# Attention rows through memory in a perceiver layer on one Trainium2 core

## The reference

```python
def _layernorm(x): return (x - mean(x)) / sqrt(var(x) + eps)

def xattn(query, key, value):                       # 16 heads of 16
    Q, K, V = heads(query @ Wq.T + bq), heads(key @ Wk.T + bk), heads(value @ Wv.T + bv)
    scores = softmax(einsum('bhsd,bhtd->bhst', Q, K) / sqrt(16), axis=-1)
    out = einsum('bhst,bhtd->bhsd', scores, V)
    out = out.reshape(B, T_src, D_MODEL)            # (b, h, s, d) read as rows, heads not put back
    return out @ Wh.T + bh

def attn(x):                                        # random features, causal sums
    q, k, v = split(x @ Wqkv + bqkv)
    qf, kf = features(q), features(k)               # normalise, project, clip, exp
    ctx = einsum(qf, cumsum(kf x v)); den = maximum(einsum(qf, cumsum(kf)), 1e-6)
    out = (ctx / den).transpose(0, 2, 1, 3).reshape(B, T, C)
    return out @ Wout + bout

def ffn(x): return (silu(x @ wg.T) * (x @ wu.T)) @ wd.T

x = x + xattn(_layernorm(x), ctx_1024, ctx_1024)
x = x + attn(_layernorm(x))
x = x + ffn(_layernorm(x))                          # weights int / 127
```

## Time and profile before

| | |
|---|---|
| median of three runs | 876.47 us |
| profiled execution | 875.48 us, span 873.8 us |
| PE busy | 829.1 us (95%) |
| ACT busy | 541.5 us (62%) |
| DVE busy | 417.2 us (48%) |
| granted PE clock, mean | 0.99 |
| mean DMA rate | 137 GB/s |

### The profile page before, as it was taken

How to read it: one execution, slowest core, us unless ns; L and a number is a source line. 1 busy time by engine, 2 the same in 40 slices (tenths; PEclk the granted TensorE clock), 3 DMA queues, 4 the chain that set the end, 5 groups by cost and what they waited for, 6 DMA issues and landing times.

```text
span 873.8 us, 20543 instructions
## 1 busy us (share of the span) xinstructions
PE 829.1 (95%) x8817; PEld 569.8 (65%) x8817; DVE 417.2 (48%) x746; ACT 541.5 (62%) x598; POOL 47.1 (5%) x76
## 2 busy tenths in 40 slices
PE   6899999999999998999999998999999999989876
PEld 5666666666666666676666665667666666657656
DVE  7433236444644445534654446354474444402654
ACT  2478887776577665667567764575657666672141
POOL 1034000000000000000000000000000000000010
PEclk9899999999999999999999999999999999999999
DMA  7486654646344333346343441443614333202000
GB/s 248 172 258 237 241 183 166 209 158 193 122 146 146 142 125 133 122 133 191 136 146 145 146 142 53 158 158 129 195 65 170 122 122 119 100 2 50 0 2 15
DMA packets 58768, 120.08 MB, mean 137 GB/s; under 512 B 21552, under 2 KB 29744, under 8 KB 55152
## 3 DMA queue, kind: packets, MB, share of 16 engines
q1 hardware_dynamic: 56880, 114.31, 38.3%
q0 software_dynamic: 1792, 4.40, 1.7%
HBM read 78.84 MB, written 37.75 MB: 133 GB/s over the span
## 4 chain that ended last, share of the span: by engine, by line
PE 82%; DVE 8%; issue 4%; DMA 2%; ACT 2%; DVEq 1%; POOL 1%; SPq 0%; POOLq 0%; ACTq 0%
PE ps_o L816 26%; PE ps_s L828 18%; PE ps_pa L662 10%; PE ps_pa L617 10%; PE ps_pa L763 2%; PE ps_pa L692 2%; PE ps_pa L788 2%; PE ps_pa L775 2%; PE ps_pa L754 1%; ACT probs L1258 1%; PE ps_pa L740 1%; DMA oscr<-y 1%; PE ps_pa L684 1%; PE ps_pa L795 1%; PE ps_pa L767 1%
## 5 line engine op out<-in xcount | busy, mean ns | idle before, releaser
L1258 ACT ACTIVATE probs<-ps_s 128x1024 f32<-128x1024 f32 x512 | 496.8, 1023 | 234.2 <-PE ps_s L828 227.7
L816 PE MATMUL ps_o<-probs,values 128*17 128x256 f32 x4096 | 256.1, 385 | 0.0
L828 PEld LDWEIGHTS ps_s<-qstack,kstack 64*128 64x128 f32 x2048 | 140.0, 186 | 99.6 <-ACT probs L1258 48.8
L828 PE MATMUL ps_s<-qstack,kstack 64*128 64x256 f32 x2048 | 194.0, 307 | 5.3 <-ACT probs L1258 5.3
L816 PEld LDWEIGHTS ps_o<-probs,values 128*17 128x17 f32 x4096 | 104.1, 98 | 98.7 <-issue 9.8
L1343 DVE TENSOR_SCALAR kparts<-ps_pa,b_heads 128x512 fp32r<-128x512 f32 x64 | 48.0, 750 | 107.4 <-PE ps_pa L617 107.1
L662 PE MATMUL ps_pa<-wv_hi,ctx_hi 128*128 128x256 f32 x256 | 79.6, 311 | 2.9 <-DVE wv_lo L1331 2.2
L1360 DVE TENSOR_TENSOR values<-ps_pa,bv_pair 128x512 f32<-128x512 f32 x64 | 44.2, 690 | 77.5 <-PE ps_pa L662 77.1
L662 PE MATMUL ps_pa<-wv_lo,ctx_hi 128*128 128x256 f32 x256 | 72.5, 283 | 0.0
L662 PE MATMUL ps_pa<-wv_hi,ctx_lo 128*128 128x256 f32 x256 | 72.4, 283 | 0.0
L617 PE MATMUL ps_pa<-ctx_hi,wk_hi 128*128 128x512 f32 x128 | 56.4, 441 | 0.0
(11 more groups left out here) (274 smaller groups left out, 786.7 us busy)
## 6 DMA issues: line engine op xcount, KB each, us to landing
kstack<-kscr SPq DMA_DIRECT2D x96, 512.0 KB, 5.3
kscr<-kparts SPq DMA_DIRECT2D x64, 512.0 KB, 2.7
ctx_raw<-ctxT SPq DMA_DIRECT2D x32, 512.0 KB, 6.5
qstack<-qscr SPq DMA_DIRECT2D x12, 256.0 KB, 3.5
qscr<-qparts SPq DMA_DIRECT2D x4, 512.0 KB, 3.1
xh<-x SPq DMA_DIRECT2D x4, 256.0 KB, 5.4
kstack<-kstack SPq DMA_DIRECT2D x2, 512.0 KB, 6.0
qstack<-ksample SPq DMA_DIRECT2D x4, 256.0 KB, 3.6
```

The costliest lines, as they stand in the source:

```text
L816: last = mm(ps_o[32 * j:32 * j + DH + 1, g * S:(g + 1) * S], values[par][:, i, head_of_step(g, j), :], prob[:, j * S:(j + 1) * S], start=b ...
L828: last = mm(ps_s[s % 2][:, j * S:(j + 1) * S], kstack[par][rows, u, i * P:(i + 1) * P], queries[rows, u, :], start=True, stop=True)
L1258: nc.scalar.activation(probs[n % AHEAD][:, :], ps_s[n % 2][:, :], ACT.Exp, scale=float(DH) ** -0.5).then_inc(fast["exp_done"], 1)
```

## The change

Stages: `oT0`, `oT1`, `o2T0`, `o2T1`, `y2T` go. `on` (step 9) and `o2n` (92) come, both on DVE alone. The softmax output is written from `o_sb` as it is, denominator included, one DMA for each of the four row groups of 17 partitions, and read back with the queries as rows; DVE divides after the read. The linear output takes the same way, and is read back by dimension and head, denominators repeated, so that it is already transposed: `wout`'s rows are reordered to match, in eight loads of the weight instead of one. `wh` and `wout` signal after the addition; the layernorms are stages `ln1` and `ln2` of their own. `ln0T` goes from 94 to 92, `q` from 100 to 98, `wout` from 92 to 94, `ln2T` from 96 to 99, `gu0` from 99 to 100, and ACT takes the gates up to one exponential earlier. In the last tail the first two transposes are gone, SP and ACT write two groups each, and down uses the hidden columns in two fp32r parts that DVE cuts.

```diff
-AT = {"o": 1, "oT0": 3, "oT1": 4, "yT": 12, "wh": 13, "ln1T": 19, ...
+AT = {"o": 1, "on": 9, "yT": 12, "wh": 13, "ln1": 13, "ln1T": 19, ...
-      ... "pv3": 84, "o2T0": 86, "o2T1": 88, "y2T": 90, "wout": 92,
-      "ln2T": 96, "gu0": 99, "gate0": 101, ...
+      ... "pv3": 84, "o2n": 92, "wout": 94, "ln2": 94,
+      "ln2T": 99, "gu0": 100, "gate0": 101, ...
-HEAD_AT = {"ln0": 86, "ln0T": 94, "q": 100, ...
+HEAD_AT = {"ln0": 86, "ln0T": 92, "q": 98, ...
-ACT_BEHIND = {n: 1 - AT[n] % 2 if AT[n] // QUAD in WIDE_QUADS else QUAD - 1 - AT[n] % QUAD for n in FEATS + GATES}
+ACT_BEHIND = {n: 1 - AT[n] % 2 if AT[n] // QUAD in WIDE_QUADS else QUAD - 1 - AT[n] % QUAD for n in FEATS}
+ACT_BEHIND.update({n: (QUAD - 2 if AT[n] % QUAD < 2 else QUAD - 1) - AT[n] % QUAD for n in GATES})
-        oscr = scratch("oscr", [H, S, DH], FP32)
+        o2scr = scratch("o2scr", [DH + 1, H, S], FP32)
+        oscr = scratch("oscr", [ST, DH + 1, HALF, S], FP32)
+        def write_heads(eng, c, j):
+            t, e = j // CI, j % CI
+            eng.dma_start(oscr[t].rearrange("d (g e) s -> e d g s", e=CI)[e],
+                          o_sb[32 * j:32 * j + DH + 1, :, :]).then_inc(c["o_written"], 16)
...
+            def read_rows(t, landed):
+                sp.dma_start(o_rows[:, t, :, :], oscr[t].rearrange("d h (a u) -> (h a) d u", u=DH)).then_inc(landed, 16)
+            def regroup_output(c, tails):
+                wait_all((c["o_written"], tails * (16 * GH) + 16 * GH))
                 for t in range(ST):
+                    read_rows(t, c["o_in"])
+            def turn_values(c, clock, tails):
+                wait_all((c["operand"], c.at("operand", clock, "pv3")))
+                for j in range(GH):
+                    sp.dma_start(o2scr.rearrange("d (g j) s -> j d g s", j=GH)[j],
+                                 o_sb[32 * j:32 * j + DH + 1, :, :]).then_inc(c["o2_written"], 16)
+                wait_all((c["o2_written"], tails * (16 * GH) + 16 * GH))
+                sp.dma_start(o2_den, o2scr[DH:DH + 1].to_broadcast([P // H, H, S])).then_inc(c["o2_in"], 16)
+                sp.dma_start(o2_rows, o2scr[0:DH].rearrange("(i e) h s -> (e h) i s", i=CI)).then_inc(c["o2_in"], 16)
...
+                    if b and p == AT["pv3"] // STEPS:
+                        turn_values(fast, tail_of(b - 1), b - 1)
...
+            warm(ps_p, 34)
             for t in range(ST):
-                pe.wait_ge(*vector_of("o0"))
-                for g in range(G):
-                    if g == G // 2:
-                        pe.wait_ge(*scalar_of("o1"))
-                    last = nc.tensor.transpose(halves[t][:, g * P:(g + 1) * P], o_sb[:, g, t * P:(t + 1) * P], ident[:, :])
-                last.then_inc(last_product, 1)
-            warm(ps_p, 12)
...
-            warm(ps_p, 26)
...
+                pe.wait_ge(*vector_of(f"y{t}"))
+                turn_rows(halves[2 + t], t, y).then_inc(last_product, 1)
...
+                    for part in range(2):
+                        last = mm((ps_p, ps_a)[t][:, 0:D], last_part(k, part)[:, t * P:(t + 1) * P], wd_r[:, k, :],
+                                  start=k + part == 0, stop=k + part == HB)
...
-            for dst, src in ((wh_sb, whT), (wout_sb, wout)):
-                pool.dma_start(dst[:, :, :], wr(src)).then_inc(late_in, 16)
+            pool.dma_start(wh_sb[:, :, :], wr(whT)).then_inc(late_in, 16)
+            for e in range(P // H):
+                pool.dma_start(wout_sb[e * H:(e + 1) * H, :, :], wout.rearrange("(h i e) n -> e h i n", i=CI, e=P // H)[e]
+                               ).then_inc(late_in, 16)
...
+            for j in range(CI, GH):
+                write_heads(act, fast, j)
...
+            def scaled_rows(t):
+                return v.tensor_tensor(y[:, t, :].rearrange("p (u d) -> p d u", d=DH), o_rows[:, t, 0:DH, :],
+                                       rden[:, t, :].unsqueeze(1).to_broadcast([P, DH, DH]), ALU.mult)
...
+                elif name == "on":
+                    dve.wait_ge(c["o_in"], clock[1] * (16 * ST) + 16 * ST)
+                    if c is fast and tails:
+                        dve.wait_ge(c["stored"], tails * 16)
+                    v.reciprocal(rden[:, :, :], o_rows[:, :, DH, :])
+                    check_rows()
+                    for t in range(ST):
+                        last = scaled_rows(t)
+                elif name == "o2n":
+                    dve.wait_ge(c["o2_in"], clock[1] * 32 + 32)
+                    v.tensor_scalar(o2_den, o2_den, 1e-6, None, ALU.max)
+                    dve.drain()
+                    v.reciprocal(o2_den, o2_den)
+                    dve.drain()
+                    last = v.tensor_tensor(xT[:, :, :], o2_rows, o2_den.unsqueeze(1).to_broadcast([P, CI, S]), ALU.mult)
                 elif name in ("wh", "wout"):
-                    v.tensor_tensor(xs[:, :, :], xs[:, :, :], bank[:, :].rearrange("p (t d) -> p t d", t=ST), ALU.add)
-                    dve.drain()
+                    last = v.tensor_tensor(xs[:, :, :], xs[:, :, :], bank[:, :].rearrange("p (t d) -> p t d", t=ST), ALU.add)
+                elif name in ("ln1", "ln2"):
                     last = layernorm(c, name, clock)
...
+            for t, landed in enumerate(((fast["o_in"], (B - 1) * (16 * ST) + 16), (o_in_last, 16))):
+                dve.wait_ge(*landed)
+                v.reciprocal(rden[:, t, :], o_rows[:, t, DH, :])
+                dve.drain()
+                scaled_rows(t).then_inc(last_vector, 1)
...
-                v.scalar_tensor_tensor(hid[:, k, :], gate_e[:, k % 2, :], 1.0, hid[:, k, :], ALU.add, ALU.mult
-                                       ).then_inc(last_vector, 1)
+                v.scalar_tensor_tensor(hid[:, k, :], gate_e[:, k % 2, :], 1.0, hid[:, k, :], ALU.add, ALU.mult)
+                dve.drain()
+                if k >= HALF // 2:
+                    dve.wait_ge(*product_of(f"gu{HB - 1}"))
+                cut(last_part(k, 0), last_part(k, 1), hid[:, k, :]).then_inc(last_vector, 1)
```

More of the change, by code:

```diff
@@ L542, in _ @@
             load_x(fast, B - 1, (fast["operand"], fast.at("operand", tail_of(B - 2), "down")))
-            for t in range(ST):
-                sp.wait_ge(*vector_of(f"y{t}"))
-                sp.dma_start(oscr[:, t * P:(t + 1) * P, :].rearrange("h s d -> s h d"),
-                             y[:, t, :].rearrange("p (h d) -> p h d", h=H)).then_inc(fast["o_written"], 16)
-            sp.wait_ge(fast["o_written"], B * 32)
+            sp.wait_ge(*vector_of("o0"))
+            sp.wait_ge(*scalar_of("o1"))
+            for j in range(CI):
+                write_heads(sp, fast, j)
+            sp.wait_ge(fast["o_written"], B * (16 * GH))
             for t, landed in enumerate((fast["o_in"], o_in_last)):
-                sp.dma_start(y[:, t, :], oscr[t * HALF:(t + 1) * HALF, :, :].rearrange("a (u s) d -> (a u) (s d)", u=S // DH)
-                             ).then_inc(landed, 16)
+                read_rows(t, landed)
             for t in range(ST):
@@ L723, in stage @@
                                   ident[:, :], start=True, stop=True, skip_group_check=True)
-                elif kind in ("oT", "o2T"):
-                    for g in range(G):
-                        last = nc.tensor.transpose(bank[:, g * P:(g + 1) * P], o_sb[:, g, n * P:(n + 1) * P],
-                                                   ident[:, :])
                 elif name == "yT":
-                    pe.wait_ge(c["o_in"], clock[1] * 16 + 16)
-                    last = transpose_blocks(bank, y)
-                elif name == "y2T":
                     last = transpose_blocks(bank, y)
@@ L786, in down_part @@
                 for t in range(ST):
-                    last = mm(bank[:, t * D:(t + 1) * D], hid[:, k, t * P:(t + 1) * P], wd_sb[:, k, :],
+                    last = mm(bank[:, t * D:(t + 1) * D], hid[:, k, t * P:(t + 1) * P], wd_r[:, k, :].bitcast(FP32),
                               start=k + t == 0, stop=k == HB - 1, skip_group_check=True)
@@ L1178, in _ @@
             pool.wait_ge(fast["k_stacked"][1], 3 * STACKED)
-            pool.dma_start(wd_sb[:, :, :].bitcast(INT32), wr(wdT)).then_inc(i_in, 16)
+            for k, part in zip((0, HB - CI), wd_int):
+                n = part.shape[1]
+                pool.dma_start(part, wr(wdT)[:, k:k + n, :]).then_inc(i_in, 16)
             def weighted(c, f, clock):
@@ L1412, in normalise @@
-                by_half = bank[:, :].rearrange("p (g a e c) -> p a g e c", a=CI, e=CI, c=32)
-                scale = rden[:, :].rearrange("p (g a e) -> p a g e", a=CI, e=CI)
-                for a in range(CI):
-                    last = v.tensor_tensor(y[:, t, a * P:(a + 1) * P].rearrange("p (g e d) -> p g e d", e=CI, d=DH),
-                                           by_half[:, a, :, :, 0:DH],
-                                           scale[:, a, :, :].unsqueeze(3).to_broadcast([P, G, CI, DH]), ALU.mult)
@@ L1418, in normalise @@
-                return last
```

(11 more changed lines are left out.)

141 lines of the change are left out of this document (50 added, 91 removed), and 4 rows, old and new, of the table AT.

## The result

| | median, us | lowest to highest | against before |
|---|---|---|---|
| before | 877.28 | 875.84 to 879.27 (4 runs) | |
| after | 958.25 | 957.4 to 959.67 (4 runs) | 1.0923, interval 1.0894 to 1.0951 |

The changed kernel is 81 us slower; the prediction was 965, with 860 to 985 as its range. The profiled execution took 957.4 us around a span of 955.7.

What follows compares the result with a forecast made beforehand. PE was taken to bound the kernel, busy 829.1 of 873.8 us. From 875.5, gains of 11.8 give 863.7; one-engine writes add 82 and six clock falls 20, making 965 us, range 860 to 985.

Steps and rivals of the forecast that it cites:

- One engine: Output writes: 17 partitions put each set on one DMA engine, 13.2 us a set, 82 us of waits together; chance 0.62.
- Clock falls: PE's long waits at six places in the tails: one clock fall each at 3.3 us, 20 us together.
- the 2.68 us stand: PE's stand in tail 1 of the kernel before, taken as the length beyond which the clock falls.
- The base, 863.7: Whole kernel if writes are as quick as those now: the parts sum to -11.8 us, giving 863.7 us.
- four writes go out at 198.4 and land near 202.7: Softmax rows in tail 0, spread writes: reads land at 207.9 and yT starts at 210.2, where it was.
- Setup: Batch 0: eight more weight loads on POOL at about 0.5 us each cost nothing, or 4 us once if uncovered.
- Rival 2: Tails: writes spread but late, PE standing 2 us longer at six places with clock falls, 895 us; chance 0.07.
- Sums and norms apart: ln0T in tails 0 and 1: stalls of 2.3 and 2.7 us go, and tail 1's clock fall of 3.3.
- The linear path: Late in the tails, with spread writes: wout can start at 537.4, PE wants it at 536.7, a 0.7 us stall.
- The reciprocal of 256 columns: DVE's o2n before wout: taken as 1.7 us if the excess is per column, 0.5 if fixed.
- The last batch: With spread writes wh could start 2.4 us earlier, but warming ends near 801 and a clock fall offsets it: 0.
- The gated stage: Last batch's gate and down products: DVE's four operations make a step of 1.86 us instead of 1.82, +2.7 us.

Runs made afterwards that it cites:

- e6: Changed kernel with 55 and 45 unused warming products filling PE's waits before yT and wout: 946.49 us, ratio 1.079.
- e9: Changed kernel with 32-partition writes, last batch's down product in fp32 and the softmax tail latest (on 12, yT 16): 881.93 us, ratio 1.0035.
- e2: Changed kernel with each write padded from 17 to 32 partitions, 15 of them rows nobody reads: 885.37 us, ratio 1.0077.
- e5: Kernel before with only sums and norms taken apart and ln0T moved ahead of wout, transposes kept: 868.34 us, ratio 0.9906.
- e10: Changed kernel with each write padded from 17 to 25 partitions: 899.35 us, ratio 1.0225.
- e3: Changed kernel with each write padded from 17 to 18 partitions, one row nobody reads: 884.86 us, ratio 1.0078.
- e8: Changed kernel with 32-partition writes, a later softmax tail (on 12, yT 14) and the last batch's down product in fp32: 878.75 us, ratio 1.0004.
- e11: Kernel before with sums and norms apart, and only the linear rows through memory in 32-partition writes: 868.14 us, ratio 0.9877.

## Why the prediction was right, and where its sizes were off

The step on which it rested, all 272 pieces of a set on one DMA engine, was right, and so was its cause, the count of 17. From one copy of o to the next, in the profiles, against the prediction's own terms (in each tail 12.2 and 11.0 us of waits and two clock falls, less what the tail gains):

| stretch | before | after | more | predicted |
|---|---|---|---|---|
| start to copy of o, batch 0 | 195.1 | 196.0 | 0.9 | 0 |
| to the next copy | 202.7 | 226.3 | 23.6 | 26.2 |
| to the next | 206.7 | 225.4 | 18.7 | 21.3 |
| to the last batch's | 192.4 | 216.8 | 24.4 | 27.4 |
| to the end | 76.8 | 91.1 | 14.3 | 14.8 |
| sum | 873.8 | 955.7 | 81.9 | 89.7 |

- **One engine.** Predicted 48 ns a piece (40 to 54) and 13.2 us a set; the windows give 43 ns, 11.7 us. PE stands 13.1 us before yT, where the 12.2 counted and the 1.1 by which PE is early make 13.3; 10.5 before wout, where 11.0 and the stall of 0.7 make 11.7; 11.5 before the last yT (12.1 for the chain). The sizes hold within 1.2 us, in part by luck: the set took less than thought, and the queueing ahead of it and the reads behind it more. Three slips in the working hardly matter to it: 272 pieces at 48 ns are 13.1 us, 40 ns take 15 us off the seven sets and not 17, and the old writes of y had 4,096 pieces of 64 B, not 4,352.
- **Clock falls.** 3.3 us each was too much; e6 gives 2.0. Over six this is 8 us, and it is nearly the whole distance between 965 and 958. This is the term of the total that was mis-sized: 3.3 was 3.0 of lost work in one stretch and an allowance for its edges. Why a fall costs less here was not shown. Nor is the 2.68 us stand a border: in e9 the clock fell behind a stand of 1.94.
- **The base, 863.7, was wrong as the time with spread writes, and it did not show in the total.** e2 has the spread writes and takes 885. What was wrong is "four writes go out at 198.4 and land near 202.7": they go out behind 1.5 MB for the key stack and 256 KB of xs, and it takes 7.9 us, not the 4.3 that a set takes with nothing ahead of it. Three tails at 4.0 us of wait and 2.0 of clock (e6's price, for a longer stand) are 18 of the 21 us. In e2's profile the three tails lie 6.1, 6.7 and 7.3 us above the prediction's stretches for spread writes, the end 0.9; another 3.8 lie ahead of the first copy of o (see Setup). The missing time stayed hidden since on one engine the wait is there anyway: from e2 to after the ratio moves by 0.0846, 74 us, where the prediction put 82 + 20 = 102. That is 28 too much, against 21 too little in the base, and the 7 left over is the distance of 965 from 958. PE's waits tell the same: those before yT, wout and the last yT are 82.9 us in after and 15.8 in e2, and three more clock falls at 2.0 make the step 73. As the time with no such waits at all, 863.7 fits: with 82.9 and six falls of 2.0 it gives 958, an estimate. Rival 2 had the shape of the softmax half (spread, but late, a clock fall each), though not the cause, which it put in the 64 B reads or the reciprocal, and I gave it 0.07. It would have been the main case had the partitions been 32.
- **Sums and norms apart.** Right: e5 confirms its gain, 9.5 us against its own before. No wait of PE on a layernorm is left in the tails.
- **The linear path.** The 0.7 us wait of wout on spread writes: 0.8 in two tails of e2, 0.5 in the third. The reciprocal of 256 columns, predicted 1.7 us from the excess of one with 16:

```profile
356.21 0.29 DVE L1545 TENSOR_SCALAR feat<-feat 128x256 f32<-128x256 f32 x1 [10.74 <-DMA feat<-o2scr]
...
356.58 1.75 DVE L1547 RECIPROCAL feat<-feat 128x256 f32<-128x256 f32 x1
...
359.76 3.78 PE L727 MATMUL ps_pa<-wout_sb,xT 128*128 128x256 f32 x8 [10.66 <-DVE xhT L1476]
```

  The excess is per column (with 32 columns 0.35: 6.25 ns for each more). The estimate of 2.1 us by the Trainium skill's repeat count ("VectorE: DVE Perf Modes", section "Walkthrough: the 8-slice pipeline in each mode") lies above it; the measurement decides.
- **The last batch.** The warming products do not end near 801. At 0.23 us each, 34 last 7.86 us, about as long as the spread chain, so that PE's longest wait for y there is 0.9 us in e2; in the kernel after, on one engine, PE stood 11.5 behind them. I had read one instruction as one product.
- **The gated stage.** Predicted +2.7. From the first gate product, 937.46, to the start of the output's sum it is 11.04 us against 9.17 before: +1.9. The step between the products is 1.71 us (before 1.82 between the down sums, set by PE), not 1.86: four DVE operations of 1.54 us, and what lies between them is less than I gave the drains.

```profile
937.46 0.42 DVE L1795 TENSOR_TENSOR amat<-kfeat,ps_s 128x256 f32<-128x256 f32 x1 [1.97 <-ACT kfeat L1339]
...
940.97 0.41 DVE L1795 TENSOR_TENSOR amat<-kfeat,ps_o 128x256 f32<-128x256 f32 x1
...
942.68 0.41 DVE L1795 TENSOR_TENSOR amat<-kfeat,ps_o 128x256 f32<-128x256 f32 x1
...
948.50 0.76 DVE L1804 SCALAR_TENSOR_TENSOR y<-ps_pa,xs 128x256 f32<-128x256 f32 x2 [0.59 <-PE ps_pa L1025]
```

- **Setup.** No cost of the eight loads is seen: the first copy of o is 0.9 us later here. It lies between 195.4 and 198.9 in the padded kernels, which have the same loads, and its place goes with PE's granted clock from 30 to 40 us: 1.00 in before (195.1) and e10 (195.4), 0.95 in after (196.0), 0.83 in e3 (197.8), 0.57 in e2 (198.9). e5, without the loads, has 0.97 and 196.0. So up to some 3.8 us of a profiled execution are the clock of the setup, not the change.

Open: that the loads ahead make e2's set late rests on the comparison of its softmax and linear sets (7.9 against 4.4 us), no run took the loads away; and whether a better order of the tail would make the softmax rows through memory pay at all. Three places of it were tried, and the transposes that it saves are worth about 1 us a tail.

## What to carry to other kernels

Look at the partition count of every DMA before its bytes: a count with no divisor from 2 to 16, as the 17 here, puts the whole transfer on one engine, and writing rows that nobody reads is far cheaper than that (958 to 885 us here, and one row more does as well as fifteen). The time of a hop through memory is made of the issue, the traffic already on the engines at that moment, and the read's own time, not of the bytes over the bandwidth: read the share of the windows ahead of its issue. And when a wait is moved, look for the next one: e9 has none of the 7 us that PE waited before yT in e8, and is no faster, whereas freeing one transpose from a norm that it did not need (e5, e11) gave 9 to 10 us.

## What the runs showed that I had not expected

- SP is held while it issues to a single engine: four writes of 68 KB occupied its queue for 8.59 us, spread ones of 128 KB for 3.29 (late in the tail, with no load ahead: 5.99 and 2.52). What stands behind them in SP's order is late by that too.
- One fall of TensorE's clock after a stand of over 10 us costs 2.0 us, by the medians, and 4.1, 4.0 and 4.7 us for the two falls of a tail, by the profiles of e6 and of the kernel after. But the clock also fell behind waits of about 2 us, in two of the three tails of e9 (the first at 249.42), so that a short wait may cost as much again.
- In e8's profile, waits of up to 2.7 us stood before yT in all three tails, and a mean clock below 0.95 only behind the first. The profiled execution, 873.27 us, is the fastest of its 873.27 to 880.92; its first copy of o is early too (195.7, clock 0.97 from 30 to 40 us). That the spread comes from the number of falls in each execution and from the clock of the setup would fit; it wasn't shown.
